# Attention with fp32 probabilities and values, and half of the softmax row sums added on GpSimd

## The reference

```python
# x: (2, 1024, 1024) fp32; 32 heads of 32; Wqkv: (3072, 1024); Wout, weight_real: (1024, 1024)
xn = (x - mean(x)) / sqrt(var(x) + 1e-5)
qkv = clip(xn @ Wqkv.T, -8, 8)
q, k, v = split(qkv)
q, k = layer_norm(q) * q_ln_w + q_ln_b, layer_norm(k) * k_ln_w + k_ln_b
scores = q @ k.T / sqrt(32) + slope[head] * (pos_k - pos_q)      # per head
scores = where(pos_k <= pos_q, scores, -1e30)
attn = (softmax(scores) @ v) @ Wout.T
ffn = xn @ (mean(abs(W)) * sign(W)).T + bias
out = x + attn + ffn
```

## Time and profile before

| | us |
|---|---|
| median of 3 runs (lowest, highest) | 1599.47 (1593.47, 1602.29) |
| the profiled execution's own time | 1597.0 |
| its span, first to last instruction | 1595.2 |
| PE busy / its mean granted clock | 1434.3 (90%) / 0.972 |
| DVE busy | 870.1 (55%) |
| POOL (GpSimd) busy | 755.4 (47%) |
| ACT (ScalarE) busy | 582.1 (36%) |

### The profile page before, as it was taken

How to read it: one execution, slowest core, us unless ns; L and a number is a source line. 1 busy time by engine, 2 the same in 40 slices (tenths; PEclk the granted TensorE clock), 3 DMA queues, 4 the chain that set the end, 5 groups by cost and what they waited for, 6 DMA issues and landing times.

```text
span 1595.2 us, 29109 instructions
## 1 busy us (share of the span) xinstructions
PE 1434.3 (90%) x11560; PEld 698.2 (44%) x11560; DVE 870.1 (55%) x1326; ACT 582.1 (36%) x1065; POOL 755.4 (47%) x412
## 2 busy tenths in 40 slices
PE   4899999999999989998888887888888788889998
PEld 2455445444545434444344443344444344434443
DVE  6665355545455323476677667677776777631111
ACT  4443133323333211115555455455554455540000
POOL 4221122222222100007777777777777678894443
PEclk9999999999999999999999999989999999999999
DMA  6453232323232482111222222212222221025443
GB/s 235 150 164 115 64 79 60 79 60 76 63 79 59 93 219 73 67 53 48 69 63 69 65 66 66 59 29 69 63 70 69 62 63 30 22 82 166 158 144 121
DMA packets 145415, 137.15 MB, mean 86 GB/s; under 512 B 83744, under 2 KB 112416, under 8 KB 145120
## 3 DMA queue, kind: packets, MB, share of 16 engines
q1 hardware_dynamic: 48285, 90.80, 17.9%
q10 hardware_dynamic: 97027, 44.89, 11.7%
HBM read 93.06 MB, written 42.47 MB: 85 GB/s over the span
## 4 chain that ended last, share of the span: by engine, by line
PE 63%; issue 10%; DVE 10%; DMA 5%; POOL 4%; ACTq 3%; SPq 2%; ACT 2%; POOLq 0%; DVEq 0%
PE ps L957 38%; PE ps L1118 7%; PE ps L1032 5%; PE ps L1093 5%; DVE arena L893 4%; PE ps L1123 3%; DVE arena L831 3%; POOL arena L546 2%; DMA arena<-r_scr 2%; PE ps L1010 2%; ACT arena L666 2%; DVE arena L886 2%; DMA r_scr<-arena 1%; SPq L425 1%; PE ps L1096 1%
## 5 line engine op out<-in xcount | busy, mean ns | idle before, releaser
L957 PE MATMUL ps<-arena 128*128 128x512 f16 x3584 | 793.6, 381 | 14.5 <-ACT arena L593 5.4
L546 POOL TENSOR_TENSOR arena<-arena 128x2048 f16<-128x2048 f32 x192 | 543.8, 2856 | 344.9 <-ACT arena L666 344.7
L957 PEld LDWEIGHTS ps<-arena 128*128 128x128 f16 (+1 forms) x3584 | 349.4, 98 | 429.4 <-issue 10.0
L831 DVE TENSOR_REDUCE arena<-ps 128x1 f16<-128x512 f32 (+3 forms) x768 | 381.8, 549 | 186.2 <-PE ps L1035 119.8
L666 ACT ACTIVATE arena<-ps 128x512 f32<-128x512 f32 (+3 forms) x768 | 333.0, 492 | 271.4 <-PE ps L1096 201.9
L1032 PE MATMUL ps<-arena 127*128 127x512 f16 (+3 forms) x768 | 246.0, 342 | 57.2 <-DVE arena L831 55.0
L1093 PE MATMUL ps<-arena 128*128 128x512 f16 (+3 forms) x768 | 248.9, 341 | 41.6 <-ACT arena L666 40.0
L1118 PE MATMUL ps<-arena 128*32 128x512 bf16 (+7 forms) x3072 | 227.1, 342 | 20.2 <-ACT arena L674 11.8
L802 DVE TENSOR_SCALAR arena<-ps 128x1024 f32<-128x1024 f32 x48 | 58.8, 1225 | 206.4 <-PE ps L957 206.4
L1093 PEld LDWEIGHTS ps<-arena 128*128 128x128 f16 x768 | 75.9, 100 | 144.3 <-issue 59.1
L1123 PE MATMUL ps<-arena 128*32 128x512 bf16 (+7 forms) x1536 | 134.4, 339 | 0.0
(11 more groups left out here) (50 smaller groups left out, 889.6 us busy)
## 6 DMA issues: line engine op xcount, KB each, us to landing
arena<-in_x SPq DMA_DIRECT2D x32, 512.0 KB, 4.9
arena<-in_wqkv_t SPq DMA_DIRECT2D x48, 256.0 KB, 4.0
base_scr<-arena SPq DMA_DIRECT2D x16, 512.0 KB, 2.9
q_scr<-arena ACTq DMA_DIRECT2D x16, 512.0 KB, 4.1
k_scr<-arena ACTq DMA_DIRECT2D x16, 512.0 KB, 4.5
v_scr<-arena SPq DMA_DIRECT2D x16, 512.0 KB, 2.9
arena<-r_scr SPq DMA_DIRECT2D x128, 64.0 KB, 2.0
arena<-base_scr SPq DMA_DIRECT2D x16, 512.0 KB, 4.0
```

Of the source, the lines that this page charges most:

```text
L546: nc.gpsimd.tensor_tensor(pl[k % PSLOTS][:, :, 0:w], p32[k % PSLOTS][:, :, 0:w], ph[k % PSLOTS][:, :, 0:w], ALU.subtract).then_inc(pl_done, 1)
L831: ins = nc.vector.tensor_reduce(negm[s % 2][:, at:at + 1], ps[:, NATB[use(s, pos) % RB], col:col + width], AX, ALU.max, negate=True)
L957: ins = nc.tensor.matmul(dst[c], lhs(k, a), wparts[:, k, b, c * HALF:(c + 1) * HALF], start=(k == 0 and (a, b) == order[0]), stop=(k == KT ...
```

## The change

P stays fp32 as the exponential wrote it, and V is stored in fp32 as it was clipped (scaled by SW, which the constant `ones_w`, set to SW, puts into the row sums too). A chunk has one fp32 product with V per head. `v_scr` has the same number of bytes as before, as has `vg`. ScalarE's and DVE's split of V goes.

Row sums are made in two ways. In the four chunks of qb 0 and the first of qb 1 (`DIRECT`) PE multiplies P with ones as well. In the chunks of qb 1 with t from 2 to 7 GpSimd adds P into `acc` (the first of these adds the P of t = 1 and t = 2); one product with ones after the last chunk's product takes in `acc`. GpSimd thus has six additions per group in place of twelve subtractions. There are four slots for P. `rb` becomes the second half of `os_sb`.

The diff, cut (pool names and semaphores that only go are left out):

```diff
-        PSLOTS = 3
+        PSLOTS = 4
...
+        DIRECT = [qb == 0 or t == 0 for qb, t in CHUNKS]
+        ADDS = QT - 2
+
+        def adds_for(k):
+            n, (qb, t) = k // NC, CHUNKS[k % NC]
+            return ADDS * n + (max(1, t - 1) if qb == 1 and t > 0 else 0)
...
             def store_v(t, p):
-                sp.wait_ge(vl_done, ready(t))
+                sp.wait_ge(mm_out, ready(t + NT * V))
...
             for n in range(GROUPS):
                 for c in range(NC):
+                    qb, t, at, w = span(c)
                     k = n * NC + c
-                    w = span(c)[3]
+                    if DIRECT[c] or t == 1:
+                        continue
                     pool.wait_ge(exp_done, GH * (k + 1))
-                    nc.gpsimd.tensor_tensor(pl[k % PSLOTS][:, :, 0:w], p32[k % PSLOTS][:, :, 0:w],
-                                            ph[k % PSLOTS][:, :, 0:w], ALU.subtract).then_inc(pl_done, 1)
+                    if t == 2:
+                        need(pool, pv_done, n * NC)
+                    need(pool, add_done, adds_for(k) - 1)
+                    before = p32[(k - 1) % PSLOTS] if t == 2 else acc[:, :, at:HALF]
+                    nc.gpsimd.tensor_tensor(acc[:, :, at:HALF], before, p32[k % PSLOTS][:, :, 0:w], ALU.add)\
+                      .then_inc(add_done, 1)
...
-                act.wait_ge(mm_out, ready(t + NT * V))
-                act.wait_ge(v_st[p], stored(j))
-                nc.scalar.activation(vst[p][:, :, 0, :], xc[p].rearrange("p (h d) -> p h d", h=HEADS),
-                                     ACT.Copy, scale=1.0 / SW).then_inc(vh_done, 1)
...
                 if j == 0:
                     need(act, pv_done, k - PSLOTS + 1)
+                    need(act, add_done, adds_for(k - PSLOTS))
...
-                dve.wait_ge(vh_done, slot_free(t))
-                clipped(t + NT * V, p)
+                dve.wait_ge(v_st[p], stored(j))
+                clipped(t + NT * V, p, vst)
                 split_lo(WO, t, p, j)
-                dve.wait_ge(vh_done, ready(t))
-                nc.vector.scalar_tensor_tensor(vst[p][:, :, 1, :],
-                                               xc[p].rearrange("p (h d) -> p h d", h=HEADS),
-                                               1.0 / SW, vst[p][:, :, 0, :], ALU.mult, ALU.subtract)\
-                  .then_inc(vl_done, 1)
...
-                pe.wait_ge(pl_done, k + 1)
+                p, v = p32[k % PSLOTS], vg[n % 2]
+                pe.wait_ge(exp_done, GH * (k + 1))
...
-                for part in (hi, lo):
-                    for s in range(2):
-                        for j in range(GH):
-                            ins = nc.tensor.matmul(dst(O_BANK, j), v[:, t, j, s, :], part[:, j, 0:w],
-                                                   start=first and part is hi and s == 0,
-                                                   stop=last and part is lo and s == 1)
-                        if s == 0:
-                            for j in range(GH):
-                                nc.tensor.matmul(dst(S_BANK, j), ones16, part[:, j, 0:w],
-                                                 start=first and part is hi, stop=last and part is lo)
+                for j in range(GH):
+                    ins = nc.tensor.matmul(dst(O_BANK, j, at), v[:, t, j, :], p[:, j, 0:w], start=first, stop=last)
+                if DIRECT[c]:
+                    for j in range(GH):
+                        ins = nc.tensor.matmul(dst(S_BANK, j, at), ones_w, p[:, j, 0:w],
+                                               start=first, stop=last and qb == 0)
+                if last and qb == 1:
+                    pe.wait_ge(add_done, ADDS * (n + 1))
+                    for j in range(GH):
+                        ins = nc.tensor.matmul(dst(S_BANK, j, 0), ones_w, acc[:, j, :], start=False, stop=True)
                 ins.then_inc(pv_done, 1)
```

More of the change, by code:

```diff
@@ L121, in build_program @@
         alpha = f32(vst_at, DM)
-        vst = [f16(vst_at + s * DM, 2 * DM).rearrange("p (h s d) -> p h s d", h=HEADS, s=2)
-               for s in range(2)]; at += 2 * DM
+        vst = [f32(vst_at + s * DM, DM) for s in range(2)]; at += 2 * DM
         ln_at = at
@@ L136, in build_program @@
         ks = [f16(a + GH * SEQ // 2, GH * SEQ).rearrange("p (j t) -> p j t", j=GH) for a in stack_at]
-        PSLOTS = 3
+        PSLOTS = 4
         PW = GH * HALF
         at = XNT_AT
-        p32, ph, pl = [], [], []
-        for s in range(PSLOTS):
-            p32.append(f32(at, PW).rearrange("p (j q) -> p j q", j=GH))
-            ph.append(f32(at, PW).bitcast(BF16)[:, 1:2 * PW:2].rearrange("p (j q) -> p j q", j=GH))
-            pl.append(f16(at + PW, PW).rearrange("p (j q) -> p j q", j=GH))
-            at += PW + PW // 2
-        vg = [f16(at + s * DM, 2 * DM).rearrange("p (t j s d) -> p t j s d", t=QT, j=GH, s=2)
-              for s in range(2)]; at += 2 * DM
+        p32 = [f32(at + s * PW, PW).rearrange("p (j q) -> p j q", j=GH) for s in range(PSLOTS)]; at += PSLOTS * PW
+        acc = f32(at, PW).rearrange("p (j q) -> p j q", j=GH); at += PW
+        vg = [f32(at + s * DM, DM).rearrange("p (t j d) -> p t j d", t=QT, j=GH) for s in range(2)]; at += 2 * DM
         os_sb = [f32(at + s * DM, DM).rearrange("p (a q) -> p a q", a=2) for s in range(2)]; at += 2 * DM
-        rb = [f32(at + s * HALF, HALF) for s in range(2)]; at += DM
+        rb = [os_sb[s][:, 1, :] for s in range(2)]
         ot_at = [W1_AT + s * DM for s in range(12)] + [at + s * DM for s in range(2)]
@@ L162, in build_program @@
         rout = [f32(at + s * 16, 16) for s in range(2)]; at += 32
-        ones16 = f16(at, DH); at += DH // 2
+        ones_w = f32(at, DH); at += DH
         assert at <= WORDS, at
@@ L559, in _ @@
         def _(act):
-            for s in (w_hi, xn_done, xh_done, xth_out, hi_done, qt_out, vh_done):
+            for s in (w_hi, xn_done, xh_done, xth_out, hi_done, qt_out):
                 act.sem_inc(s, RING)
@@ L708, in _ @@
         def _(dve):
-            for s in (w_lo, stats, xl_done, xtl_out, mm_out, u_done, vl_done):
+            for s in (w_lo, stats, xl_done, xtl_out, mm_out, u_done):
                 dve.sem_inc(s, RING)
@@ L796, in _, with clipped @@
                 f_out(NT - 2 + p, p, NT // 2 - 1)
-            def clipped(g, p):
+            def clipped(g, p, dst):
                 dve.wait_ge(mm_done, g + 1)
                 lim = CLIP * SX * SW
-                nc.vector.tensor_scalar(xc[p], banks(2 * p, 2), lim, -lim, ALU.min, ALU.max)\
+                nc.vector.tensor_scalar(dst[p], banks(2 * p, 2), lim, -lim, ALU.min, ALU.max)\
                   .then_inc(mm_out, 1)
@@ L811, in qk_step @@
                     w, b = ln_w[LNQ[blk]], ln_b[LNQ[blk]]
-                    clipped(g, p)
+                    clipped(g, p, xc)
                     dve.wait_ge(mm_out, ready(g))
```

20 lines of the change are left out of this document (8 added, 12 removed).

## The result

The change is slower: 1637.4 us (median of 4, 1635.3 to 1640.7), beside 1600.9 us for the kernel before; the ratio is 1.0256 with a 95% interval from 1.023 to 1.0283. The forecast was 1762, with the range 1510 to 1855: the side was right, the size and, as follows, the reason were wrong, so that the side came out right was luck. The profiled execution took 1640.7 us, its span 1638.9, against 1597.0 and 1595.2.

The account below looks back on a forecast made before the run. Attention was taken as bound by PE, with gaps from DVE, ScalarE and, through DVE, GpSimd. 1597 + 240 + 9 - 75 - 7 - 2 = 1762 us; range 1510 to 1855, the likeliest case alone 1687 to 1855.

Parts of the forecast that it names:

- PE starts instructions in the order of its program: Narrow fp32 products: only neighbouring heads' instructions overlap, so four heads take 5 x 0.43 us instead of 2 x 0.43.
- The term of +240 us: Narrow products on PE in attention: 28.4 instead of 13.4 us per group, +15.0 us over 16 groups.
- The weight loads, +9: Fp32 weight loads on PE outlast a 128-wide step; 14 such steps per group, +9 us (0 to 18).
- What comes back: PE's idle time and clock loss in attention: 5.0 of 9.3 us per group return, -75 us (0 to -140).
- The last group, -7: Last attention group, without maxima, PE idle for 8.0 of its 34 us: -7 us.
- Edits at nothing: V stage's dropped copy and subtraction count only at its end, -2 us; V's bytes, fourth P slot, new waits nothing.
- The fourth slot at nothing: Fourth P slot in attention: costs nothing, and no wait on a slot shows now.
- The margin: Additions end about 21 us after the seventh chunk's exponentials; needed after over 30 us, or 24 at 41 us per group.
- Full overlap: Rival, 0.25: four heads' narrow instructions run side by side whatever their order, -7 us there; 1539 us (1504 to 1574).
- its relief of 51 us: Full overlap's gain from less GpSimd work: fewer DVE delays, waits for GpSimd, clock loss, and the start.
- Full overlap, and GpSimd gives it back: Rival, 0.07: additions 1 us longer than subtractions still meet two DVE operations per group, eating the gain; about 1597 us.

Follow-up runs that it names:

- f1: Kernel before, loop over heads put outside, so each head's three narrow products follow each other on the same columns; 1592.9 us, one execution.
- e4: Changed kernel without the V products of three heads in each group's sixth chunk, two in the seventh, one in the eighth; 1631.5 us, one execution.
- e3: Changed kernel with four buffers for the clipped V in place of two (xc beside vst); 1629.7 us, 1.0193 of before.
- e7: Changed kernel with three slots for P in place of four; 1641.1 us, 1.031 of before.
- e2: Changed kernel, DVE's first-half normalization and second-half low half moved into the next group's first chunks, ScalarE's o_high along; 1552.9 us, 0.9707 of before.
- e1: Changed kernel without GpSimd's additions and the waits for them, the summed P a constant; 1547.6 us, 0.9695 of before.
- e5: Changed kernel, each GpSimd addition cut into four of one head, DVE's places unchanged; 1562.2 us, 0.9801 of before.
- e6: Changed kernel with all row sums made on PE by products with ones, no GpSimd in attention; 1588.9 us, 0.9965 of before.
- e14: Changed kernel with DVE's two operations moved, four V buffers, ScalarE's transfers spread, all row sums on PE, no GpSimd additions; 1544.8 us, 0.9712 of before.
- e13: Changed kernel with DVE's two operations moved, four V buffers, ScalarE's transfers spread over chunks, additions cut per head; 1513.2 us, 0.9502 of before.

## Why the prediction was wrong

- **"PE starts instructions in the order of its program"**, and from it five steps of 0.43 us for four heads, is the step that failed. The step length was right (0.43 to 0.45), the factor is 2. The term of +240 us should have been about -7 by two steps; PE's own work moved by -0.3 us per group, about -5 in all. f1 shows that the order of the program does not hold products on other columns; e4 shows it for the pairs. The rows read before could not tell: all of them rotate over the heads. That was said, and 0.55 was put on it all the same.
- **The weight loads, +9:** loads of 32 fp32 columns took 0.11 us each, not the 0.19 of 128 columns, and no chunk shows a gap for them. Zero.
- **"What comes back", -75:** nothing came back. The idle time was expected to shrink because PE would get slower; PE did not, and idle time and clock together rose from 9.1 to 12.4 us per group. GpSimd's hold on DVE was seen in the rows and priced as relief, by its total (34 to 21 us per group). What counts is the length of one instruction and where it lies: 4.66 us in place of 3.71, at the place where `o_norm` and `o_low` stand. DVE's two kinds of operation lost 83 us to GpSimd before and 92 with the change.
- **The last group, -7:** from its first exponentials to its last it takes 31.3 us in place of 33.5, -2.
- **"Edits at nothing", -2:** the end of the V stage did get better (the 4.77 us of the earlier trace rows are 2.52), but the slack of a tile that `xc` gave was a cover. Its loss costs some 10 us at the stage's start, the clock included (728.2 for the first exponentials against 717.8 in e3): +6 in all. The fourth slot at nothing was right (e7), and so were the new waits at this pace: PE waits nowhere for additions, and ScalarE 3.6 us in the whole kernel. The margin was as thin as it said: at 41 us per group, in e2, ScalarE waits 35 us for them.
- **The rivals.** *Full overlap* (0.25) had the narrow work right and its relief of 51 us wrong. *Full overlap, and GpSimd gives it back* (0.07) had the mechanism, with a wait 1 us longer per meeting, but ended at no change: it left out that PE's clock falls behind the longer stands. Idle time +1.3 and clock +2.0 us per group are what it missed.

Shown by undoing one part: the meeting of additions and DVE (e1, e5; e2 moved ScalarE's `o_high` too), the V buffers (e3), the slots (e7). The kernel before has such meetings as well, with its subtractions. What they cost there was not measured by leaving them out, so how the 2.6% comes out as a difference of the two is read from the traces. The clock was not varied by itself: its share is read from the windows, and it was above that of the change in every run that took long pauses out of attention.

## What to carry to other kernels

A GpSimd operation that meets DVE operations with two inputs costs by its length, not by its sum: keep the two apart in time first, and cut the long one where that can't be done. Less work on GpSimd in longer pieces can be worse. On a dense TensorE a pause of some microseconds is to be priced at more than itself, since the granted clock falls behind it (here 1.3 us more idle time per group came with 2.0 us of clock); and removing a copy also removes the buffer that it filled, so look who writes and stores there next.

## What the runs showed of the hardware

- Narrow fp32 products: two instructions per product, 0.43 to 0.45 us each at 512 columns, for one head as for four. Products in different column groups run side by side in both orders of the program that were tried, sets that rotate over the heads and one head after the other (1.44 and 1.46 us for 24 products).
- A DVE operation of 0.68 us took up to 4.86 us beside a GpSimd addition (4.66 in the mean), and in the two meetings shown ended 0.54 and 0.55 us after it.
- More work in place of pauses did not lower TensorE's clock: 473 us busy of 580 at 0.90 (the change), 529 at 0.97 (e6), 542 at 1.00 (e14). All 27 falls in the fourteen groups of the change lie in or right behind stands of 2.3 to 4.5 us.
- Open: what causes the remaining waits in e13 (PE behind the additions, 16 us, and behind one late DVE place, 16 us, in the stretch), and by which path narrow products pass each other.
